# A Toeplitz product with only the corner blocks off the diagonal: 32x32 array tiles inside a stream of 128x128 passes

## The chip, the core and the metric

The kernel runs on one core of a Trainium2 chip. A core has a matrix engine (PE; its weight loads are shown as PEld), a vector engine (DVE), a scalar engine (ACT), GpSimd (POOL) and SyncE (SP), which run their own instruction streams and wait for each other by semaphores. Matmul results land in eight PSUM banks, `ps[0]` to `ps[7]`, each 128 partitions by 512 fp32. The metric is device time of one execution in microseconds (us), median of a few runs. A measurement of this kernel tells a change from no change at about 0.3%.

## The reference, cut to what matters

The whole program is a chain of small blocks (a deformable convolution, a Fourier-domain convolution, a Nystrom attention, a mixture of experts, a linear attention, a routed transformer). The change is in the Nystrom attention, in its residual term: a convolution of the values `v` along the tokens, one filter of 33 taps per head.

```
v: (b, h, n, dh), here 8 images, 8 heads, 256 tokens, 16 columns per head
pad = 33 // 2
res = conv_general_dilated(v, res_w, padding=((pad, pad), (0, 0)), feature_group_count=h)
out = a1 @ pinv(a2) @ (a3 @ v) + res          # pinv: 6 Newton-Schulz steps
```

Token i of `res` takes tokens i-16 to i+16 of `v`. With the 256 tokens in two blocks of 128, block t of the result needs all of block t of `v`, and of the other block the 16 tokens next to the border.

## The kernel before

Everything is written out by hand, engine by engine, in the order in which each engine executes it; semaphores `S[...]` tie the streams together. There is no scheduler: an engine that waits holds all that stands behind it.

The convolution is done as a matrix product. `toepb[:, h, 0:384]` holds head h's banded Toeplitz matrix (128 partitions, three column blocks of 128); block t of the result from block s of `v` uses its columns `(1 - t + s) * 128` on. The result comes out with its tokens reversed, which is undone later (`turn_residual`, line 776, with a flip matrix). The moving operand is `Vb[:, :, s, head]`, 8 images x 16 columns = 128 columns.

On PE, lines 743 to 749: for each t, each head h, each s one 128x128 product of 128 columns. That is 2 x 8 x 2 = 32 products. Every fp32 product is two passes in the trace, so there are 64 passes. Bank `ps[2t + h//4]` holds four heads; the banks complete in the order 0, 1, 2, 3, each with `res_mm` + 1.

On ACT, lines 1166 to 1170, a loop of four turns: wait for `a1_sub`, take the exponential of one 512-column piece of `a1` (line 1169), then `residual(n)` waits for `res_mm`, copies bank n out of PSUM (line 1159) and signals `res_ev`. Behind the loop stand four small scalings (`linear_term`, line 1164), and behind them the copies of the first Newton-Schulz step (line 1178), which DVE waits for.

On DVE, lines 1526 to 1533, a loop of four turns makes `a1_sub` (a maximum, line 1529, and a subtraction, line 1530, on banks 4 to 7) and from the second turn on sums the exponentials of the turn before (lines 1523, 1524). After it comes the Newton-Schulz step (lines 1547 to 1558).

On PE behind the residual products stands `pinv_step(0, ...)`: four groups of products (line 759) into banks 0 to 3, group q only when `res_ev` says that its bank has been copied out. Then line 765, which waits for DVE. The middle steps run in a loop, in which PE also turns a piece of the residual (line 776). GpSimd stages the first piece when `res_ev` is 4 (line 486).

Of the kernel before, what the change touches and what calls it, by code (L numbers as in the profile page):

```python
# [25 lines left out]
P = 128  # L26
BI, BG, PT = 4, 2, 2
# [3 lines left out]
HEADS, DH, LM = 8, 16, 16  # L31
# [93 lines left out]
def build(nc, x, cst, w32, par, rows, toep, w_out, moe_w1, moe_w2, moe_b2, am, fm, codes, rec_a, rec_b, out):  # L125
    ctx = ExitStack()
    with ctx:
# [3 lines left out]
        S = {n: ctx.enter_context(nc.semaphore(n)) for n in SEMS}  # L131
        ps = [ctx.enter_context(nc.psum_tensor(f"ps{i}", [P, 512], F32))[:, :] for i in range(8)]
# [76 lines left out]
        toepb = sb("toepb", HEADS * 384).rearrange("p (h n) -> p h n", h=HEADS)  # L209
# [311 lines left out]
        def _(pe):  # L521
            mm = nc.tensor.matmul
# [22 lines left out]
            for g in range(BG):  # L545
                for k in range(KK):
                    last = mm(ps[g][0:BI * NOFF, 0:N], off_bd[:, k, :, :], window(xnp, g, k // 3, k % 3, 16),
                              start=(k == 0), stop=(k == KK - 1))
                last.then_inc(S["off_mm"], 1)
            pe.wait_ge(S["off_ev"], BG)  # L550
            for t in range(PT):
                for g in range(BG):
                    c0 = (t * BG + g) * BI * NOFF
                    last = tr(ps[2][:, c0:c0 + BI * NOFF],
                              offC[0:BI * NOFF, g * N + t * P:g * N + t * P + P],
                              ident[0:BI * NOFF, 0:BI * NOFF])
# [4 lines left out]
            for r in range(BG * PT):  # L561
                for bi in range(BI):
                    if 0 < r <= PT:
                        pe.wait_ge(S["g_ev"], (r - 1) * BI + bi + 1)
                    elif r:
                        pe.wait_ge(S["g_evD"], (r - 1 - PT) * BI + bi + 1)
                    mm(ps[4 + bi][:, 0:KK * C], xn[:, r * P:r * P + P], dcn_bd[:, bi, :],
                       start=True, stop=True).then_inc(S["g_mm"], 1)
# [43 lines left out]
            for k in range(KK):  # L612
                for g in range(BG):
                    last = mm(ps[0][64 * g:64 * g + 64, 0:N], conv_bd[:, k, :, :],
                              window(xp, g, 3 * (k // 3), 3 * (k % 3), 16), start=(k == 0), stop=(k == KK - 1),
                              skip_group_check=True)
# [3 lines left out]
            for t in range(PT):  # L620
                last = tr(ps[2][:, t * P:t * P + P], feat[:, t * P:t * P + P], ident)
# [5 lines left out]
            for t in range(PT):  # L627
                last = mm(ps[3], featT[:, t, :], dft[:, t, 0:2 * N], start=(t == 0), stop=(t == PT - 1))
# [8 lines left out]
            for g in range(BG):  # L637
                for t in range(PT):
                    mm(ps[1][:, (t * BG + g) * P:(t * BG + g + 1) * P],
                       x1C[:, g * N + t * P:g * N + t * P + P], ident, start=False, stop=False,  # L640
                       skip_group_check=True)
            keep_busy(4)
            pe.wait_ge(S["gated"], 2)
            for a in range(2):
                for t in range(PT):
                    last = tr(ps[7][:, (a * PT + t) * P:(a * PT + t + 1) * P],
                              gated[:, a * N + t * P:a * N + t * P + P], ident)
            last.then_inc(S["fft_mm"], 1)
            pe.wait_ge(S["fft_ev"], FFT_EV["gT"])
            for n, (a, t) in enumerate(((0, 0), (0, 1), (1, 0), (1, 1))):  # L650
                last = mm(ps[2], gT[:, a, t, :], dft[:, t, a * N:a * N + 2 * N], start=(n == 0), stop=(n == 3))
# [4 lines left out]
            for n, src in enumerate((outf, gatef)):  # L656
                pe.wait_ge(S["abs"], n + 1)
                for t in range(PT):
                    last = mm(T1[:, t, :, n * CH:n * CH + CH], src[:, t * P:t * P + P],
                              ident.rearrange("p (b c) -> p b c", b=B), start=False, stop=True,  # L660
                              skip_group_check=True)
# [29 lines left out]
            for b in range(B):  # L691
                last = mm(ps[0][:, 16 * b:16 * b + 16], ql_bd[:, b, :, :], kl[:, b, :], start=True, stop=True)
            last.then_inc(S["sim2_mm"], 1)
            for bi in range(BI):
                pe.wait_ge(S["v_ev"], bi + 1)
                for g in range(BG):
                    last = mm(ps[4 + bi][:, g * N:g * N + N], ql_bd[:, 2 * bi + g, :, :],
                              kT[:, 512 * bi + N * g:512 * bi + N * g + N], start=True, stop=True)
                last.then_inc(S["sim3_mm"], 1)
            for bi in range(BI):  # L700
                pe.wait_ge(S["a3_exp"], bi + 1)
                for j in range(4):
                    last = tr(ps[4 + bi][:, j * P:j * P + P], a3[:, 512 * bi + j * P:512 * bi + j * P + P], ident)
                last.then_inc(S["a3T_mm"], 1)
            for bi in range(BI):
                pe.wait_ge(S["a3T_ev"], bi + 1)
                for g in range(BG):
                    b = 2 * bi + g
                    for t in range(PT):
                        c0 = 512 * bi + (g * PT + t) * P  # L710
                        last = mm(ps[2 + b // 4][:, (b % 4) * P:(b % 4) * P + P], a3T[:, c0:c0 + P],
                                  V[:, c0:c0 + P], start=(t == 0), stop=(t == PT - 1))
# [3 lines left out]
            for b in range(B):  # L716
                last = tr(ps[b // 4][:, (b % 4) * P:(b % 4) * P + P], bdX[:, b, :, :], ident)
# [4 lines left out]
            for half in range(2):  # L722
                pe.wait_ge(S["xT_ev"], half + 1)
                for j in range(4):
                    b = half * 4 + j
                    last = mm(ps[half][:, j * P:j * P + P], bdXT[:, b, :, :], bdXT[:, b, :, :],
                              start=True, stop=True)
                last.then_inc(S["y0_mm"], 1)
            pe.wait_ge(S["cr_in"], 1)
            for bi in range(BI):  # L730
                for g in range(BG):
                    for t in range(PT):
                        c0 = 512 * bi + g * N + t * P
                        last = mm(ps[4 + bi][:, (g * PT + t) * P:(g * PT + t + 1) * P], qT[:, c0:c0 + P],
                                  kl_bd[:, 2 * bi + g, :, :], start=True, stop=True)
# [3 lines left out]
            Vb = V.rearrange("p (b t n) -> p b t n", b=B, t=PT)  # L739
            pe.wait_ge(S["y_bd"], 2)  # L740
            pe.wait_ge(S["w3_ev"], 1)
            for t in range(PT):
                for h in range(HEADS):
                    for s in range(PT):
                        col = (1 - t + s) * P
                        last = mm(ps[2 * t + h // 4][:, (h % 4) * P:(h % 4) * P + P], toepb[:, h, col:col + P],
                                  Vb[:, :, s, h * DH:h * DH + DH], start=(s == 0), stop=(s == PT - 1))
                    if h % 4 == 3:
                        last.then_inc(S["res_mm"], 1)

# [2 lines left out]
            def pinv_step(it, meanwhile, bank_free=lambda q: None):  # L753
                for q in range(4):
                    bank_free(q)
                    pe.wait_ge(S["y_bd"], it * 4 + 3 + q)
                    for j in range(2):
                        b = 2 * q + j
                        last = mm(ps[q][:, 160 * j:160 * j + 160], bdY[:, b, :], YV[:, b, :], start=True, stop=True)  # L759
                    last.then_inc(S["yy_mm"], 1)  # L760
                meanwhile(it)
                for q in range(4):
                    pe.wait_ge(S["rest_set"], it * 4 + 1 + q)
                    for j in range(2):
                        last = mm(ps[q][:, 320 + 64 * j:384 + 64 * j], bdY2[:, 2 * q + j, :, :],  # L765
                                  pG[:, 2 * q:2 * q + 2, :], start=True, stop=True)
                    last.then_inc(S["wy_mm"], 1)
# [17 lines left out]
                                  ident)  # L785
                    last.then_inc(S["a1T_mm"], 1)

            pinv_step(0, nothing, lambda q: pe.wait_ge(S["res_ev"], q + 1))
            pe.wait_ge(S["a1_sub"], BI)
            with pe.Fori(1, PINV - 1) as it:  # L790
                pinv_step(it, turn_residual)
# [2 lines left out]
            for b in range(B):  # L794
                pe.wait_ge(S["y_bd"], 4 * PINV + 3 + b // 2)
                last = mm(ps[b // 4][:, (b % 4) * P:(b % 4) * P + P], bdZ[:, b, :, :], w3_bd[:, b, :, :],
                          start=True, stop=True)
# [3 lines left out]
            for bi in range(BI):  # L801
                pe.wait_ge(S["w2_ev"] if bi < 2 else S["w2_evD"], 1)
                pe.wait_ge(S["a1T_ev"], BI)
                for g in range(BG):
                    b = 2 * bi + g
                    last = mm(ps[4 + bi][:, g * N:g * N + N], w2_bd[:, b, :, :], a1T[:, N * b:N * b + N],  # L806
                              start=True, stop=True)
                last.then_inc(S["oT_mm"], 1)
            pe.wait_ge(S["late_in"], LATE)
            for bi in range(BI):  # L810
                pe.wait_ge(S["oT_ev"], bi + 1)
                last = mm(ps[0][32 * bi:32 * bi + 32, :], woutb, oT[:, 512 * bi:512 * bi + 512],
                          start=True, stop=True)
            last.then_inc(S["ao_mm"], 1)
            pe.wait_ge(S["ao_ev"], 1)
            for g in range(BG):
                for t in range(PT):
                    last = mm(ps[2][:, (t * BG + g) * P:(t * BG + g + 1) * P],
                              lnC[:, g * N + t * P:g * N + t * P + P], ident, start=False, stop=True,
                              skip_group_check=True)  # L820
# [8 lines left out]
            for g in range(BG):  # L829
                last = mm(ps[1][64 * g:64 * g + 64, 0:N], gate_bd, lnC[:, g * N:g * N + N], start=True, stop=True)  # L830
# [5 lines left out]
            for t in range(PT):  # L836
                last = tr(ps[3][:, t * P:t * P + P], probs[:, t * P:t * P + P], ident)
# [3 lines left out]
            for b in range(B):  # L841
                for t in range(PT):
                    j = t * B + b
                    last = mm(ps[4][0:C, 16 * b:16 * b + 16], t0[:, j * C:j * C + C], mT[:, t, 16 * b:16 * b + 16],
                              start=(t == 0), stop=(t == PT - 1))
# [5 lines left out]
            for e in range(EXP):  # L851
                q, c = e % 4, e // 4
                last = mm(ps[5][32 * q:32 * q + B, HID * c:HID * c + HID], pooled[:, B * e:B * e + B],
                          w1b[:, HID * e:HID * e + HID], start=True, stop=True)
# [3 lines left out]
            for c in range(4):  # L858
                last = tr(ps[6][:, c * P:c * P + P], hid_rows[:, c * P:c * P + P], ident)
# [3 lines left out]
            for e in range(EXP):  # L863
                last = mm(ps[4][0:C, B * e:B * e + B], w2b[:, C * e:C * e + C], hid[:, e, 0:B],
                          start=True, stop=True)
# [17 lines left out]
            for g in range(BG):  # L883
                for t in range(PT):
                    c0 = (t * B + g * BI) * C
# [166 lines left out]
        def _(act):  # L1052
# [101 lines left out]
                   scale=small[:, 34:35]).then_inc(S["y_bd"], 1)  # L1154
            rr4 = res.rearrange("p (t b h e) -> p t h b e", t=PT, b=B, h=HEADS)

            def residual(n):
                act.wait_ge(S["res_mm"], n + 1)
                af(rr4[:, n // 2, 4 * (n % 2):4 * (n % 2) + 4],
                   ps[n].rearrange("p (h b e) -> p h b e", h=4, b=B), ACT.Copy).then_inc(S["res_ev"], 1)  # L1160

# [4 lines left out]
            for bi in range(BI):  # L1166
                act.wait_ge(S["a1_sub"], bi + 1)
                v = a1[:, 512 * bi:512 * bi + 512]
                af(v, v, ACT.Exp).then_inc(S["a1_exp"], 1)
                residual(bi)  # L1170
            act.wait_ge(S["z0_set"], 1)
            for q in range(4):
                linear_term(0, q)
# [1 line left out]
            def pinv_step(it, meanwhile, last_one):  # L1175
                for q in range(4):
                    act.wait_ge(S["yy_mm"], it * 4 + 1 + q)
                    af(bdY2[:, 2 * q:2 * q + 2].rearrange("p b h m -> p b (h m)"),
                       ps[q][:, 0:320].rearrange("p (b c) -> p b c", b=2)[:, :, 0:P], ACT.Copy
                       ).then_inc(S["yy_ev"], 1)  # L1180
                meanwhile(it)
                if not last_one:
                    for q in range(4):
                        linear_term(it + 1, q)
# [645 lines left out]
```

## Time and profile before

| | |
|---|---|
| median of 3 runs | 342.33 us (341.65 to 342.83) |
| the profiled execution: device time | 342.63 us |
| its span, first to last instruction | 340.8 us |
| mean granted TensorE clock | 0.988 |
| PE busy | 301.4 us (88%), 2034 matmul passes |
| DVE busy | 195.4 us (57%) |
| ACT busy | 159.2 us (47%) |
| the 64 passes of line 746 | 7.3 us, 144.27 to 151.6 us |

The profile gives busy time per engine, groups of instructions per line, the chain of work that ended last, and the instructions in order of time. Three things are to be kept in mind. A matmul pass is pipelined: its row lasts some 0.27 us, but in a stream the next one starts 0.11 us later, so the start times say more than the durations. A busy PE does not mean that PE sets the time. And a chain names, for each step, what came last before it; whoever is not in it had time to spare, how much has to be read from the other engines' rows.

### The profile page before, as it was taken

The numbers are of one execution on the slowest core, as the hardware profiler recorded it, in microseconds if no ns is written. First come the engines' busy times: TensorE is split into PE (matmuls) and PEld (weight loads), VectorE is DVE, ScalarE is ACT, GpSimd is POOL, SyncE is SP. The second block draws the span as 40 slices with busy tenths as digits, with TensorE's granted clock in tenths as the row PEclk, the third lists the DMA queues.
The fourth block names the chain that finished last, engine by engine and source line by source line (L and its number), as shares of the span: only waits on it lengthen the run. The fifth ranks groups of instructions, "written<-read, shape, count | busy, mean of one in ns | idle before, by whom it ended". The sixth has DMA issues, their size and how long they took to land.

```text
span 340.8 us, 6667 instructions
## 1 busy us (share of the span) xinstructions
PE 301.4 (88%) x2034; PEld 199.1 (58%) x2034; DVE 195.4 (57%) x468; ACT 159.2 (47%) x346; POOL 37.6 (11%) x34
## 2 busy tenths in 40 slices
PE   7999999999889899999999989899986887777770
PEld 3665777776444358998998346588542552234420
DVE  4585998882165775688885652723512482228520
ACT  1097677776164267365662242112043495527820
POOL 5200190001000060001200000242000000000010
PEclk9999999999999999999999999999999799999997
DMA  3944100000000000000000233331000000000001
GB/s 90 251 102 112 56 0 2 2 2 0 2 0 0 1 2 0 2 0 2 1 0 0 40 66 61 68 68 35 2 3 20 2 0 0 17 17 0 0 15 35
DMA packets 9385, 9.17 MB, mean 27 GB/s; under 512 B 4079, under 2 KB 8943, under 8 KB 9071
## 3 DMA queue, kind: packets, MB, share of 16 engines
q1 hardware_dynamic: 9096, 8.53, 11.1%
q8 instruction: 15, 0.25, 0.3%
q10 hardware_dynamic: 264, 0.30, 0.3%
q14 instruction: 10, 0.08, 0.1%
HBM read 8.57 MB, written 0.26 MB: 26 GB/s over the span
## 4 chain that ended last, share of the span: by engine, by line
PE 30%; DVE 12%; issue 5%; ACT 4%; DMA 2%; DVEq 1%; SPq 0%; POOL 0%; POOLq 0%
PE ps L759 3%; PE ps L528 3%; PE ps L765 3%; DMA recA<-rec_a 2%; PE ps L915 2%; ACT arena L1255 2%; PE ps L1034 2%; DVE rmax L1706 2%; PE ps L905 1%; PE ps L1026 1%; PE ps L897 1%; PE ps L1004 1%; PE ps L776 1%; PE ps L806 1%; DVE arena L1530 1%
## 5 line engine op out<-in xcount | busy, mean ns | idle before, releaser
L528 PE MATMUL ps<-xC,cstb 128*128 128x512 f32 (+3 forms) x140 | 59.7, 554 | 0.0
L1375 DVE TENSOR_TENSOR arena<-arena 128x512 f32 x72 | 44.4, 688 | 7.8 <-ACT arena L1086 4.5
L1093 ACT ACTIVATE arena<-ps 128x512 f32<-128x512 f32 x72 | 37.7, 602 | 15.7 <-PE ps L585 15.6
L528 PEld LDWEIGHTS ps<-xC,cstb 128*128 128x128 f32 x140 | 24.6, 190 | 24.7 <-issue 24.6
L585 PE MATMUL ps<-cstb,arena 128*128 128x128 f32 x288 | 36.3, 277 | 0.7 <-DVE arena L1375 0.7
L585 PEld LDWEIGHTS ps<-cstb,arena 128*128 128x128 f32 x288 | 31.0, 140 | 9.4 <-DVE arena L1375 8.6
L593 PE MATMUL ps<-arena 128*32 128x256 f32 x288 | 19.2, 385 | 0.0
L1255 ACT ACTIVATE arena<-ps,rmax 128x256 f32<-128x256 f32 x32 | 14.9, 471 | 5.6 <-DVE rmax L1706 5.6
L1274 ACT ACTIVATE arena<-ps,w2c 128x512 f32<-128x512 f32 x16 | 9.7, 689 | 12.9 <-PE ps L1026 12.9
L759 PE MATMUL ps<-arena 128*128 128x160 f32 x96 | 14.5, 304 | 0.3 <-DVE arena L1558 0.3
L996 PE MATMUL ps<-cstb,arena 128*128 128x128 f32 x64 | 10.5, 286 | 4.4 <-DVE arena L1714 4.2
L1706 DVE TENSOR_REDUCE rmax<-ps 128x2 f32<-128x512 f32 x16 | 10.8, 684 | 5.8 <-PE ps L985 5.8
L497 POOL TENSOR_TENSOR arena<-w32b,cstb 128x1024 f32<-128x1024 f32 x4 | 7.6, 1895 | 57.5 <-PEq L891 45.8
L759 PEld LDWEIGHTS ps<-arena 128*128 128x128 f32 x96 | 13.3, 190 | 0.5 <-DVE arena L1558 0.4
L453 POOL TENSOR_SCALAR cgw<-cstb,parb 128x128 f32<-128x128 f32 x1 | 9.6, 9605 | 30.9 <-DMA codeB<-codes 30.9
L996 PEld LDWEIGHTS ps<-cstb,arena 128*128 128x128 f32 x64 | 6.7, 140 | 10.8 <-DVE arena L1714 10.8
L1034 PE MATMUL ps<-arena,w2c 128*32 128x512 f32 x32 | 11.1, 605 | 2.0 <-ACT arena L1274 2.0
L1061 ACT ACTIVATE small<-small 128x16 f32<-128x16 f32 x5 | 1.1, 216 | 23.3 <-DVE small L1301 22.3
L506 POOL TENSOR_TENSOR ln_a<-tC,hC 128x512 f32<-128x512 f32 x1 | 1.3, 1266 | 94.9 <-DVE hC L1734 94.9
L765 PE MATMUL ps<-arena,bdY 128*128 128x64 f32 x96 | 11.5, 273 | 0.3 <-DVE arena L1549 0.3
L765 PEld LDWEIGHTS ps<-arena,bdY 128*128 128x128 f32 x96 | 11.2, 192 | 0.5 <-DVE arena L1549 0.5
L992 PE MATMUL ps<-cstb 128*128 128x256 f32 x32 | 9.8, 387 | 1.9 <-ACT arena L1255 1.9
(374 smaller groups left out, 542.8 us busy)
## 6 DMA issues: line engine op xcount, KB each, us to landing
arena<-rec_a SPq DMA_DIRECT2D x19, 128.5 KB
toepb<-toep SPq DMA_DIRECT2D x1, 1536.0 KB
w32b<-w SPq DMA_DIRECT2D x1, 1225.0 KB
cstb<-cst SPq DMA_DIRECT2D x1, 1044.0 KB
recA<-rec_a SPq DMA_DIRECT2D x4, 128.5 KB
arena<-rec_b SPq DMA_DIRECT2D x19, 16.5 KB
w1b<-moe_w SPq DMA_DIRECT2D x1, 264.0 KB
xC<-x SPq DMA_DIRECT2D x1, 256.0 KB, 2.8
```

The costliest lines, as they stand in the source:

```text
L528: mm(ps[bank][:, 0:cols], ident if lhs is None else lhs, (xC if rhs is None else rhs)[:, 0:cols], start=True, stop=True)
L585: last = tr(ps[c % BI][:, (q * PT + t) * P:(q * PT + t + 1) * P], ST[:, c, t, q * 8:q * 8 + 8, :], ident)
L593: last = mm(ps[4 + g][32 * bi:32 * bi + 32, 0:N], GS[:, g, q, bi, k, :], SQ[:, g * BI + bi, q, :], start=False, stop=last_one and q == PT - 1,
L759: last = mm(ps[q][:, 160 * j:160 * j + 160], bdY[:, b, :], YV[:, b, :], start=True, stop=True)
L765: last = mm(ps[q][:, 320 + 64 * j:384 + 64 * j], bdY2[:, 2 * q + j, :, :], pG[:, 2 * q:2 * q + 2, :], start=True, stop=True)
L992: mm(ps[a][:, 0:N], ident, cstb[:, 0:N], start=True, stop=True)
L996: last = tr(ps[a][:, (u * PT + t) * P:(u * PT + t + 1) * P], pr[:, a * 512 + t * N + u * P:a * 512 + t * N + u * P + P], ident)
L1034: last = mm(ps[1][32 * bi:32 * bi + 32, :], w2c[:, 0:C], f1[:, 512 * bi:512 * bi + 512], start=True, stop=True)
L1093: af(SQ[:, c].rearrange("p q n -> p (q n)"), ps[c % BI], ACT.Copy).then_inc(S["s_ev"], 1)
L1255: last = af(pr[:, b * 512 + t * N:b * 512 + t * N + N], ps[b][:, t * N:t * N + N], ACT.Exp, bias=rmax[:, 2 * b + t:2 * b + t + 1], accum_o ...
L1375: tt_(ST[:, c], hy.unsqueeze(3).to_broadcast([P, PT, 16, 16]), hx.unsqueeze(2).to_broadcast([P, PT, 16, 16]), ALU.mult).then_inc(S["prod"], 1)
L1706: v_.tensor_reduce(rmax[:, 2 * b:2 * b + 2], arr3(ps[b], N), AX.X, ALU.max, negate=True).then_inc(S["sc_max"], 1)
```

## The change

The product of a whole off-diagonal block is replaced by a 32-row corner of it: of block 1-t only the 32 tokens `edge` next to the border are taken, and only the 32 rows of the result that can need them are written. The operands lie on 32 partitions, the result on 32 partitions: a tile of 32x32 of the matrix array, the one at rows and columns 0 to 31 for t = 0, the one at 96 to 127 for t = 1.

The loops are turned: head outside, then the two whole products (t = 0, 1) and then the two corners. So banks 0 and 2 fill together in heads 0 to 3, banks 1 and 3 in heads 4 to 7. ACT copies the banks out in the order 0, 2, 1, 3, still one per turn of its loop, and PE waits in the first Newton-Schulz step for `res_ev` of 1, 3, 3, 4 in place of 1, 2, 3, 4.

```diff
-            for t in range(PT):
-                for h in range(HEADS):
-                    for s in range(PT):
-                        col = (1 - t + s) * P
-                        last = mm(ps[2 * t + h // 4][:, (h % 4) * P:(h % 4) * P + P], toepb[:, h, col:col + P],
-                                  Vb[:, :, s, h * DH:h * DH + DH], start=(s == 0), stop=(s == PT - 1))
+            for h in range(HEADS):
+                cols = slice((h % 4) * P, (h % 4) * P + P)
+                for t in range(PT):
+                    mm(ps[2 * t + h // 4][:, cols], toepb[:, h, P:2 * P], Vb[:, :, t, h * DH:h * DH + DH],
+                       start=True, stop=False, skip_group_check=True)
+                for t in range(PT):
+                    edge = slice(96 * t, 96 * t + 32)
+                    c0 = (2 - 2 * t) * P + edge.start
+                    last = mm(ps[2 * t + h // 4][edge, cols], toepb[edge, h, c0:c0 + 32],
+                              Vb[edge, :, 1 - t, h * DH:h * DH + DH], start=False, stop=True, skip_group_check=True)
                     if h % 4 == 3:
                         last.then_inc(S["res_mm"], 1)
 
-            pinv_step(0, nothing, lambda q: pe.wait_ge(S["res_ev"], q + 1))
+            pinv_step(0, nothing, lambda q: pe.wait_ge(S["res_ev"], (1, 3, 3, 4)[q]))
 
-            def residual(n):
-                act.wait_ge(S["res_mm"], n + 1)
+            def residual(turn, n):
+                act.wait_ge(S["res_mm"], turn + 1)
...
-                residual(bi)
+                residual(bi, (0, 2, 1, 3)[bi])
```

On PE, the residual products of before, with the banks they write (each row is that many products, two passes each):

```order
L734 MATMUL ps7<-kl_bd,arena 128x128 x4
L746 MATMUL ps0<-arena,toepb 128x128 [waits w3_ev,y_bd,late_in]
L746 MATMUL ps0<-arena,toepb 128x128 x7
L746 MATMUL ps1<-arena,toepb 128x128 x8
L746 MATMUL ps2<-arena,toepb 128x128 x8
L746 MATMUL ps3<-arena,toepb 128x128 x8
L759 MATMUL ps0<-arena 128x160 [waits y_bd,res_ev,z0_set]
```

And the same place after the change, its first two heads (line 745 is the whole product, line 750 the corner; eight such groups of four follow each other, the last four on banks 1 and 3):

```order
L745 MATMUL ps0<-arena,toepb 128x128 [waits w3_ev,y_bd,late_in]
L745 MATMUL ps2<-arena,toepb 128x128
L750 MATMUL ps0<-arena,toepb 32x128
L750 MATMUL ps2<-arena,toepb 32x128
L745 MATMUL ps0<-arena,toepb 128x128
L745 MATMUL ps2<-arena,toepb 128x128
L750 MATMUL ps0<-arena,toepb 32x128
L750 MATMUL ps2<-arena,toepb 32x128
```

The number of products stays at 32; half of them are now corners, and the stream changes between whole-array products and 32-row tiles fifteen times, a sixteenth time where line 759 of before follows.

On ACT, the loop of four turns before:

```order
L1169 ACTIVATE arena<-arena 128x512 [waits a1_sub]
L1159 ACTIVATE arena<-ps0 128x4x8x16 [waits res_mm]
L1169 ACTIVATE arena<-arena 128x512 [waits a1_sub]
L1159 ACTIVATE arena<-ps1 128x4x8x16 [waits res_mm]
L1169 ACTIVATE arena<-arena 128x512 [waits a1_sub]
L1159 ACTIVATE arena<-ps2 128x4x8x16 [waits res_mm]
L1169 ACTIVATE arena<-arena 128x512 [waits a1_sub]
L1159 ACTIVATE arena<-ps3 128x4x8x16 [waits res_mm]
L1164 ACTIVATE arena<-arena 128x64 [waits v_new,z0_set]
```

And after:

```order
L1173 ACTIVATE arena<-arena 128x512 [waits a1_sub]
L1163 ACTIVATE arena<-ps0 128x4x8x16 [waits res_mm]
L1173 ACTIVATE arena<-arena 128x512 [waits a1_sub]
L1163 ACTIVATE arena<-ps2 128x4x8x16 [waits res_mm]
L1173 ACTIVATE arena<-arena 128x512 [waits a1_sub]
L1163 ACTIVATE arena<-ps1 128x4x8x16 [waits res_mm]
L1173 ACTIVATE arena<-arena 128x512 [waits a1_sub]
L1163 ACTIVATE arena<-ps3 128x4x8x16 [waits res_mm]
L1168 ACTIVATE arena<-arena 128x64 [waits v_new,z0_set]
```

The rows are the same but for the bank: the third copy takes bank 1, and so stands ahead of the fourth exponential with a bank that fills only in PE's last four heads.

## Rows read from the trace of the kernel before

**Rows 1.** Chain of waits, 143 to 157 us: start us, us, what.
```profile
144.27 0.70 DVE small L1529
...
149.26 0.60 DVE small L1523
...
150.82 0.70 DVE arena L1530
...
151.54 0.10 ACT arena L1169
...
152.08 0.58 ACT arena L1159
...
153.24 0.28 ACT bdY L1178
...
153.62 0.22 DVE arena L1547
```
**Rows 2.** ACT in order of time: start us, us, what, count [idle before <-releaser].
```profile
146.26 0.60 ACT L1159 ACTIVATE arena<-ps 128x512 f32<-128x512 f32 x1
147.04 0.63 ACT L1169 ACTIVATE arena<-arena 128x512 f32<-128x512 f32 x1 [0.19 <-DVE arena L1530]
148.05 0.60 ACT L1159 ACTIVATE arena<-ps 128x512 f32<-128x512 f32 x1 [0.37 <-PE ps L746]
...
151.54 0.63 ACT L1169 ACTIVATE arena<-arena 128x512 f32<-128x512 f32 x1 [1.11 <-DVE arena L1530]
152.08 0.58 ACT L1159 ACTIVATE arena<-ps 128x512 f32<-128x512 f32 x1
152.56 0.68 ACT L1164 ACTIVATE arena<-arena 128x64 f32<-128x64 f32 x4
153.14 1.19 ACT L1178 ACTIVATE bdY<-ps 128x256 f32<-128x256 f32 x4
```
**Rows 3.** PE in order of time, 135 to 200 us.
```profile
144.27 7.31 PE L746 MATMUL ps<-arena,toepb 128*128 128x128 f32 x64
151.42 2.34 PE L759 MATMUL ps<-arena 128*128 128x160 f32 x16
154.03 2.00 PE L765 MATMUL ps<-arena,bdY 128*128 128x64 f32 x16 [0.27 <-DVE arena L1549]
156.34 2.59 PE L759 MATMUL ps<-arena 128*128 128x160 f32 x16 [0.31 <-DVE arena L1558]
```
**Rows 4.** Line 746 alone: count, duration ns min/median/max, first and last start.
```profile
L746 PE MATMUL ps<-arena,toepb x64: 275/275/275, 144.3 to 151.3; 128*128 128x128 f32 x64
```
**Rows 5.** PE, 57.7 to 58.1 us: whole passes (L585), then 32-column tiles (L593).
```profile
57.47 0.38 PE L585 MATMUL ps<-cstb,arena 128*128 128x128 f32 x2
57.78 0.64 PE L593 MATMUL ps<-arena 128*32 128x256 f32 x8
```
**Rows 6.** Lines 585 and 593 alone, one round.
```profile
L585 PE MATMUL ps<-cstb,arena x18: 272/273/330, 55.9 to 59.0; 128*128 128x128 f32 x18
L593 PE MATMUL ps<-arena x16: 379/379/403, 57.8 to 58.5; 128*32 128x256 f32 x16
```
**Rows 7.** PE, 205.5 to 205.9 us: tiles (L853), then a whole pass.
```profile
205.27 0.51 PE L853 MATMUL ps<-w1b,pooled 33*8 33x128 f32 x12
205.71 0.59 PE L528 MATMUL ps<-xC,cstb 128*128 128x384 f32 x1
```
**Rows 8.** Line 853 alone.
```profile
L853 PE MATMUL ps<-w1b,pooled x32: 269/269/273, 204.7 to 205.5; 33*8 33x128 f32 x32
```
**Rows 9.** PE, 190.5 to 191.05 us: the first three whole passes after an idle stretch.
```profile
190.67 0.60 PE L818 MATMUL ps<-cstb,lnC 128*128 128x128 f32 x3 [0.69 <-ACT lnC L1203]
```
**Rows 10.** PE, two idle stretches of the last part.
```profile
262.80 1.12 PE L968 MATMUL ps<-hC,arena 128*128 128x512 f32 x2 [2.57 <-DVE arena L1691]
...
303.16 1.12 PE L968 MATMUL ps<-hC,arena 128*128 128x512 f32 x2 [1.93 <-DVE arena L1691]
```
**Rows 11.** Two stretches: us, PE busy, granted clock, DMA share, GB/s.
```profile
262.00:269.00 7.00, 6.20 (x44) 0.76 0.01 2
302.00:309.00 7.00, 4.89 (x45) 1.00 0.00 1
```

## The prediction, made before the changed kernel ran

> **What bounds the kernel now.** I read the page first: PE is busy 88% of the span, so a change that takes 16 whole products off PE looks like a gain. Whether it is one, the chain of waits has to say, around 144 to 157 us. There PE does not appear at all [rows 1]: from 144.27 us the chain is DVE's loop (maximum, subtraction, sums), whose last subtraction starts at 150.82; it releases ACT's fourth exponential at 151.54, then ACT's fourth bank copy at 152.08, the four small scalings, the first copy of the Newton-Schulz step, and at 153.62 DVE again. The timeline of ACT says the same from the other side: before the fourth exponential ACT sat idle 1.11 us for DVE, and only one bank copy of the four waited for the residual products, 0.37 us at 148.05 [rows 2]. The timeline of PE shows the 64 passes from 144.27 and the next line at 151.42 [rows 3], so 7.15 / 64 = 0.1117 us a pass, though each lasts 0.275 us by itself [rows 4]. PE becomes the bound only at 156.34, where the Newton-Schulz loop begins. So a shorter residual on PE has nothing to give: the fourth exponential still waits for DVE at 151.54. It can only cost, if the banks come later than ACT asks for them.
>
> **How late ACT may get its banks.** A copy follows its exponential by 0.54 us, and the next instruction follows a copy by 0.48 us (151.54, 152.08, 152.56 [rows 2]). The fourth exponential stays at 151.54 if the third copy starts by 151.06. Before, the third copy took bank 2, the third in PE's order. Now it takes bank 1, which is complete only with the eighth and last head. From the start of a bank's last pass to ACT's copy: bank 1 of before had its 32nd pass at 144.27 + 31 x 0.1117 = 147.73, the copy started at 148.05 having waited for it [rows 2], 0.32 us. So the last head's corner must start by 150.74.
>
> **What a head costs PE now.** Before, four products, 8 passes, 0.893 us. Now 4 whole passes and 4 corner passes, with a change of array shape each way. No row of the trace has exactly this; the nearest are these.
> - Whole to tile: the last of the L585 passes starts at 57.47 + 0.38 - 0.27 = 57.58, the first tile pass at 57.78 [rows 5, 6]: 0.20 us, where in a stream it is 0.11.
> - The tile passes: eight passes of 256 columns on four column tiles; the last starts at 57.78 + 0.64 - 0.38 = 58.04, that is 0.26 after the first [rows 5, 6]. The tiles run side by side: in series eight would take 8 x 0.22. One 256-column pass is worth 0.22, so 0.04 is the first tile's load and the stagger. The twelve passes of L853, 128 columns, start within 0.51 - 0.27 = 0.24 us [rows 7, 8], two steps of 0.11 between three rounds of four. For two corners of 128 columns, two passes each: 0.11 + 0.03 = 0.14 from the first start to the last.
> - Tile to whole: the last L853 pass starts at 205.27 + 0.51 - 0.27 = 205.51, the whole pass at 205.71 [rows 7, 8]: 0.20.
> - The four whole passes: after a break the first one's weight load is not hidden. Of L818's first three passes the third starts at 190.67 + 0.60 - 0.275 = 190.995, 0.325 after the first [rows 9], and 0.11 of that is the second step: the first costs 0.213. First to fourth start: 0.213 + 2 x 0.112 = 0.437.
>
> One head: 0.437 + 0.20 + 0.14 + 0.20 = 0.977 us against 0.893. The halved array work is more than eaten by two changes of shape (0.09 above the stream's step each), the load no longer hidden (0.10), and the corners' own 0.14. The first head comes out of a running stream: last whole pass at 144.61, corners 144.81 to 144.95, the second head from 145.15. The eighth head's last corner: 145.15 + 6 x 0.977 + 0.437 + 0.20 + 0.14 = 151.79 us, 1.05 us later than ACT can bear.
>
> The Trainium skill bears on this at one place: "TensorEngine Tiling (Array Packing)", Key Properties, says that a change of tiling mode drains the engine, and its Overview gives 32x32 tiles a speedup of up to 16. By the speedup alone the corners would cost next to nothing and the time would stay at 342.3 (rival A below); by the drain the head grows. The page gives the drain no price; this trace does, about 0.09 us each way [rows 5 to 8].
>
> **The sum.** Third copy at 151.78 + 0.32 = 152.10 us; fourth exponential at 152.58 in place of 151.54: +1.04. Behind it stand on ACT the fourth copy (bank 3 long complete), four scalings and the copies for DVE, in unchanged distances, so DVE's 153.62 becomes 154.66. What else moves has time: the first copy (bank 0 complete in head four, last corner at 144.95 + 3 x 0.977 = 147.88) starts at 148.20 in place of 146.26, the second exponential at 148.68 in place of 147.04; it ends at 149.31, and DVE's second sum, at 149.2 before [rows 1], slips by 0.1 to 0.15 us, and with it the last subtraction, to 151.65: hidden below 152.58. PE goes on to line 759 at 151.98; group 0 finds its bank free, groups 1 and 2 wait for the third copy's end (152.7), group 3 for the fourth's (153.7), its last pass ends by 154.6; ACT needs it for its fourth copy at 153.14 + 0.79 + 1.04 = 154.97. Hidden. GpSimd's staging starts 1.0 later and its piece is used only after 158 us. From 154.66 on DVE and then PE run as before, all 1.04 us later.
>
> Profiled execution: 342.63 + 1.04 = 343.67. It lies 0.30 above the median of the runs, 342.33, so I give 342.33 + 1.04 = 343.4 us. I count as no change what is within 0.3%, 1.03 us: 341.30 to 343.36. The forecast lies on that edge.
>
> **Bounds.** Below: no head can make the time shorter, since DVE holds 151.54; the lowest end is a change of nothing. Above: if each corner pass were as isolated as the first pass of L818, four would cost 0.85 in place of 0.14 and 0.20, some 0.5 a head, 7 heads 3.6 us more: 347. I take 0.977, from the rows of tile passes, which are nearest.
>
> **Rivals.**
> A, not slower: the corners cost less than I think and ACT is never late. The point is exact: the last corner by 150.74 means (150.74 - 144.95) / 7 = 0.83 us a head. For it: a corner uses a sixteenth of the array, and all of my tile rows are of another shape (128 rows by 32 columns, 33 by 8). Against: it needs both drains and the load penalty halved, and both drains were the same 0.09 in two different shapes. Time 342.3.
> B: the two corners of a head don't run side by side (they differ in rows and in columns and write different banks, which no row shows together). Then two passes more in series, +0.21 a head; over seven heads 1.5 us, third copy 153.6, time 343.4 + 1.5 = 344.9. For it: nothing direct; against: column tiles overlap in rows 5 and 7.
> C: the granted clock falls once more. It fell after PE had been idle 2.57 us and stayed up after 1.93 us [rows 10]; the fall cost (1 - 0.76) x 7 = 1.7 us [rows 11]. In the new order PE's longest idle stretch here is some 0.5 us, but its array is less used. 343.4 + 1.7 = 345.1.
> D: everything after 154 us comes 1 us later, and the fall at 264 us doesn't happen in that execution: 343.4 - 1.7 = 341.7, no change. It can do so in either kernel.
>
> **How the numbers follow.** Forecast 0.66, its own range 342.9 to 343.9, half of it above 343.36. A 0.13, B 0.09, C 0.07, D 0.05. Slower: 0.33 + 0.09 + 0.07 = 0.49; same: 0.33 + 0.13 + 0.05 less what scatter takes out, 0.46; faster: 0.05, scatter of the medians alone. The range goes from 342.1 (A, with the medians' scatter) to 344.9 (B) and leaves out C, D and the far bound.
>
> **What would show it.** In the profile after: eight groups of about 0.98 us from line 745 and 750; the first idle of ACT before the first copy, until about 148.2, waiting for PE; ACT idle before the third copy, until about 152.1, waiting for PE, and none before the fourth exponential; the chain of waits going through PE's lines 745 and 750 at 145 to 152 us in place of DVE's loop; line 769's first pass at about 155.1. I am wrong if the fourth exponential still waits for DVE (A), if the heads take 1.19 (B), or if the time moves elsewhere than between 144 and 154 us.

## The result, and the profile after

The changed kernel took 344.14 us (median of 14 runs, 343.03 to 346.6) against 342.09 us of the kernel before in its 14 runs: ratio 1.0046, 95% interval 1.0023 to 1.0068, so 0.8 to 2.3 us slower. The forecast was 1.04 us slower, 343.4 us. Ratios leave out three runs, one of e2 and two of e4, that lay over 1.5% above the fastest of their kernel; the medians hold them. Its profiled execution took 343.58 us with a span of 341.8 us, 1.0 above the span of before, at nearly the same mean granted clock (0.989 to 0.988).

The chain of waits of the changed kernel, 143 to 158 us (start us, us, what), where [rows 1] had DVE's loop:

```profile
142.97 1.45 PE ps L734 x13
144.42 0.45 PE ps L745 x4
144.86 0.34 PE ps L750 x4
145.20 0.64 PE ps L745 x4
145.84 0.34 PE ps L750 x4
...
151.08 0.64 PE ps L745 x4
151.72 0.39 PE ps L750 x4
152.10 0.05 ACT arena L1163
152.15 0.43 issue
152.58 0.62 ACT arena L1173
153.20 0.49 ACT arena L1163
...
154.65 0.22 DVE arena L1551
```

The chain now runs through PE's residual, head by head, then through ACT's third bank copy and fourth exponential. ACT in order of time, the answer to [rows 2]:

```profile
145.71 0.63 ACT L1173 ACTIVATE arena<-arena 128x512 f32<-128x512 f32 x1 [3.32 <-DVE arena L1534]
148.17 0.60 ACT L1163 ACTIVATE arena<-ps 128x512 f32<-128x512 f32 x1 [1.83 <-PE ps L750]
...
152.09 0.60 ACT L1163 ACTIVATE arena<-ps 128x512 f32<-128x512 f32 x1 [1.80 <-PE ps L750]
152.58 0.62 ACT L1173 ACTIVATE arena<-arena 128x512 f32<-128x512 f32 x1
154.16 1.20 ACT L1182 ACTIVATE bdY<-ps 128x256 f32<-128x256 f32 x4
```

The copies that waited 0.37 us for PE in all now wait 1.83 and 1.80, and the fourth exponential, which had waited 1.11 us for DVE, waits for nobody: it stands behind the third copy and starts at 152.58 in place of 151.54. PE, the answer to [rows 3], two heads and the line behind:

```profile
144.25 0.61 PE L745 MATMUL ps<-arena,toepb 128*128 128x128 f32 x4
144.79 0.41 PE L750 MATMUL ps<-arena,toepb 32*32 32x128 f32 x4
145.13 0.71 PE L745 MATMUL ps<-arena,toepb 128*128 128x128 f32 x4
145.77 0.41 PE L750 MATMUL ps<-arena,toepb 32*32 32x128 f32 x4
146.11 0.71 PE L745 MATMUL ps<-arena,toepb 128*128 128x128 f32 x4
...
151.99 2.65 PE L763 MATMUL ps<-arena 128*128 128x160 f32 x16
155.06 2.00 PE L769 MATMUL ps<-arena,bdY 128*128 128x64 f32 x16 [0.43 <-DVE arena L1553]
```

A head takes 146.11 - 145.13 = 0.98 us where it had taken 0.893. Half of PE's 64 passes are now corners, and still its next line starts at 151.99 in place of 151.42.

### The profile page after: what moved, and what is told of

Same layout as the page of the kernel before. It is cut to its first block, busy times and chain, and to the rows that moved or that the text cites. A ratio compares the mean times of both kernels' runs of the same rounds, so it can differ in the third digit from the quotient of the medians.

```text
span 341.8 us, 6667 instructions
## 1 busy us (share of the span) xinstructions
PE 303.2 (89%) x2034; PEld 197.3 (58%) x2034; DVE 195.6 (57%) x468; ACT 158.9 (46%) x346; POOL 34.0 (10%) x34
## 4 chain that ended last, share of the span: by engine, by line
PE 69%; DVE 11%; ACT 9%; issue 5%; DMA 2%; DVEq 1%; POOL 1%; SPq 0%; POOLq 0%
PE ps L585 10%; PE ps L528 10%; PE ps L593 5%; PE ps L763 3%; PE ps L769 3%; DMA recA<-rec_a 2%; PE ps L547 2%; PE ps L919 2%; ACT arena L1259 2%; PE ps L1038 2%; DVE rmax L1710 2%; PE ps L745 1%; PE ps L909 1%; PE ps L1030 1%; ACT arena L1090 1%
## 5 line engine op out<-in xcount | busy, mean ns | idle before, releaser
L585 PE MATMUL ps<-cstb,arena 128*128 128x128 f32 x288 | 36.3, 277 | 0.7 <-DVE arena L1379 0.7
L585 PEld LDWEIGHTS ps<-cstb,arena 128*128 128x128 f32 x288 | 31.0, 140 | 9.4 <-DVE arena L1379 8.6
L593 PE MATMUL ps<-arena 128*32 128x256 f32 x288 | 19.2, 385 | 0.0
L1718 DVE TENSOR_TENSOR arena<-arena,rsum 128x512 f32<-128x512 f32 x16 | 11.1, 692 | 0.6
L593 PEld LDWEIGHTS ps<-arena 128*32 128x32 f32 x288 | 7.5, 109 | 6.3 <-ACT arena L1097 3.1
```

The lines of the kernel that those rows point to most:

```text
L585: last = tr(ps[c % BI][:, (q * PT + t) * P:(q * PT + t + 1) * P], ST[:, c, t, q * 8:q * 8 + 8, :], ident)
L593: last = mm(ps[4 + g][32 * bi:32 * bi + 32, 0:N], GS[:, g, q, bi, k, :], SQ[:, g * BI + bi, q, :], start=False, stop=last_one and q == PT - 1,
L1718: tt_(pb3, pb3, r.unsqueeze(2).to_broadcast([P, 2, N]), ALU.mult).then_inc(S["sc_norm"], 1)
```

## The experiments

All of them are read in two ways. One is the ratio of runs, which is blunt here. The other is two lengths out of the one profiled execution, both from the start of PE's first residual pass: to DVE's first Newton-Schulz step (line 1547 of before, "to DVE"), and to PE's products behind the last Newton-Schulz step (line 796 of before, "to the end of pinv"). In the kernel before they are 153.62 - 144.27 = 9.35 and 181.66 - 144.27 = 37.39 us [rows 1, 3]. The row of the second in the kernel before, and those of the changed kernel in its two profiles (the second profile's first residual pass is at 144.79):

```profile
181.66 2.09 PE L796 MATMUL ps<-w_bd,bdX 128*128 128x128 f32 x16
```
```profile
182.68 2.09 PE L800 MATMUL ps<-w_bd,bdX 128*128 128x128 f32 x16
```
```profile
183.23 2.09 PE L800 MATMUL ps<-w_bd,bdX 128*128 128x128 f32 x16
```

| kernel | to DVE | to the end of pinv | median us | ratio and interval |
|---|---|---|---|---|
| before | 9.35 | 37.39 | | |
| changed | 10.40 | 38.43 | 344.14 | 1.0046 (1.0023 to 1.0068) |
| e1, changed again | 10.39 | 38.44 | 342.98 | 1.002 (0.9985 to 1.0055) |
| e2, order alone | 9.46 | 37.50 | 343.02 | 1.0001 (0.997 to 1.0032) |
| e3, exponentials first | 10.00 | 38.21 | 343.30 | 1.0018 (0.999 to 1.0047) |
| e4, grouped | 9.34 | 37.37 | 342.71 | 0.9986 (0.995 to 1.0023) |
| e5, grouped, one start | 9.34 | 37.38 | 342.74 | 0.9998 (0.9974 to 1.0022) |
| e6, start early | 8.14 | 36.46 | 341.84 | 0.9966 (0.9937 to 0.9996) |
| e7, scalings early | 8.77 | 37.20 | 342.34 | 0.9982 (0.9956 to 1.0008) |
| e8, before again | 9.35 | 37.39 | 342.46 | 0.9985 (0.9956 to 1.0013) |
| e9, one corner | 10.35 | 38.38 | 340.6, one run | |
| e10, no corners | 9.33 | 39.38 | 347.98, one run | |
| e11, the same again | 9.37 | 39.52 | 345.53 | 1.010 (1.0047 to 1.0154) |
| e12, the same, filled | 9.35 | 37.39 | 342.21 | 0.9988 (0.9953 to 1.0024) |

**e1_after_again and e8_before_again**: both kernels unchanged.

> The changed kernel once more, beside the kernel before on the same chip. Its profile puts the loss at 1.04 us (DVE's first step of Newton-Schulz at 154.65 in place of 153.62), while the ratio of the runs gave 0.46%, 1.6 us. Theory P (all of it stands on the path between 144 and 154 us, the rest is scatter of the clock): ratio 1.003, between 1.002 and 1.005; over many runs the difference nears 1.04 us. Theory C (part of the loss, 0.5 us, is a TensorE clock that falls more often in the changed kernel): ratio 1.0045 or more, and a mean clock of its runs that is lower than that of the profiled one.

> The kernel before, unchanged, run as a kernel of its own, so that the granted clock of each of its runs is listed. Theory P: mean clock as that of the changed kernel's runs, 0.983, ratio 1.000. Theory C (the changed kernel's clock falls more often): its mean clock is higher, 0.986 or more, which is some 0.5 us at about 0.6 us a fall of 0.005.

The stage repeats to 0.01 us in both kernels; the rest of the span doesn't. All 26 runs of the changed kernel have a mean of 343.83 us, all 110 of the kernel before 342.68: a difference of 1.15 us with a standard error of 0.25. The clock is listed for 96 of the 110, not for the 14 of the first comparison; these 96 have a mean of 342.78 us and a mean granted clock of 0.9811, the changed kernel's 26 one of 0.9823. So theory C falls: the changed kernel's clock is no lower. The clock goes with most of the scatter: over both kernels a run is some 0.85 us longer for each 0.005 of mean clock less, and with that taken out the difference is 1.2 us, standard error 0.14. The first ratio of 1.0046, 1.6 us, was the high side of this scatter: the 14 runs of the kernel before in it had a mean of 341.94 us.

**e2_order_alone**: the changed order with whole products.

```diff
...
             for h in range(HEADS):
                 for t in range(PT):
...
+                    for s in range(PT):
+                        col = (1 - t + s) * P
+                        last = mm(ps[2 * t + h // 4][:, (h % 4) * P:(h % 4) * P + P], toepb[:, h, col:col + P],
+                                  Vb[:, :, s, h * DH:h * DH + DH], start=(s == 0), stop=(s == PT - 1))
```

> The changed order of heads, banks and copies, but both whole products for every block as before: 64 whole passes, no tile, no change of shape. Theory P: bank 1 is complete with the last head's pass 62, which starts at 144.25 + 61 x 0.112 = 151.07; third copy at 151.39, fourth exponential at 151.87 in place of 151.54: +0.33 us, ratio 1.001. Rival O (the order of banks is the whole loss, the changes of array shape cost nothing): fourth exponential at 152.6 and +1.0 us, ratio 1.003.

```profile
149.37 0.63 ACT L1169 ACTIVATE arena<-arena 128x512 f32<-128x512 f32 x1
151.24 0.60 ACT L1159 ACTIVATE arena<-ps 128x512 f32<-128x512 f32 x1 [1.24 <-PE ps L746]
151.74 0.62 ACT L1169 ACTIVATE arena<-arena 128x512 f32<-128x512 f32 x1
```

ACT in order of time: the third copy waits for PE here too, but only until 151.24, in a stage that began at 144.34. The order costs 0.11 us of the 1.04, less than the 0.33 expected; the expectation had counted bank 1's last pass as the 62nd, it is the 60th (144.34 + 59 x 0.1117 + 0.32 = 151.25), because bank 3 gets the last four. Rival O falls: the order gives ACT's wait its place, the shape changes give it its size.

**e3_exp_first**: the wait for bank 1 taken out from in front of the exponentials.

```diff
-                residual(bi, (0, 2, 1, 3)[bi])
+                if bi < 2:
+                    residual(bi, (0, 2)[bi])
+            residual(2, 1)
+            residual(3, 3)
```

> The changed kernel, but ACT takes its third and fourth exponential before the third bank copy (exponentials no longer stand behind the wait for bank 1). Theory P: the wait for PE at 152.09 is hidden behind the fourth exponential, which starts at 151.68 (DVE's last subtraction is 0.14 late); third copy 152.22, fourth 152.70, scalings 153.2 in place of 153.58 of the changed kernel: 0.4 us won back, +0.6 us against before, ratio 1.002. Rival S (PE's later stream itself sets the time, whatever ACT's order): no change against the changed kernel, +1.04 us, ratio 1.003.

To DVE 0.40 us are won back, as expected (10.00 against 10.40); to the end of pinv only 0.22. PE's last twelve passes of line 763 wait for ACT's third copy, which stands behind one more exponential here; they start 8.61 us into the stage (152.95 - 144.34), 0.12 later than in the changed kernel (152.74 - 144.25). PE goes from line 763 to line 769 with no idle time, the last pair of DVE's first step starts 0.30 us after the instruction before it (0.14 in the kernel before), and PE's next step starts 2.88 us after DVE's first step (157.22 - 154.34), 2.72 in the kernel before.

**e4_grouped and e5_grouped_one_start**: four changes of shape in place of sixteen.

```diff
...
+            for half in range(2):
+                for h in range(4 * half, 4 * half + 4):
...
+                        mm(ps[2 * t + half][:, cols], toepb[:, h, P:2 * P], Vb[:, :, t, h * DH:h * DH + DH],
+                           start=(h % 4 == 0), stop=False, skip_group_check=True)
+                for h in range(4 * half, 4 * half + 4):
...
+                        last = mm(ps[2 * t + half][edge, cols], toepb[edge, h, c0:c0 + 32],
+                                  Vb[edge, :, 1 - t, h * DH:h * DH + DH], start=False, stop=True,
...
```

The cut is e5's: it sets the start flag only on the whole products of the bank's first head, so that the corners add. e4 has `start=True` on every whole product, ahead of all corners of the bank, and its corners do not all add. The program's output is off by a relative 0.19, by more than with the corners left out altogether (0.07 in e10 below), which fits corners that replace what stands in their 32 rows. Which heads' corners do so was not looked at. e4 serves as a measurement of time alone.

> The changed kernel with the same 32 products, but per pair of banks first the eight whole products, then the eight corners: four changes of array shape in place of sixteen. Theory P: PE's residual ends near 150.1 in place of 152.0, bank 1 is ready for ACT at 150.2, the fourth exponential waits for DVE again at 151.54: the loss is gone and nothing is won, ratio 1.000 (0.998 to 1.002), the profile's line 1551 step of DVE at 153.6. Rival T (tiles of 32x32 are slow by themselves, not the changes): the corners take as long as before, the residual ends after 151.1 and some loss stays, ratio 1.001 to 1.003.

> The grouped order of before (eight whole products, then their eight corners, per pair of banks), now with the start flag only on the first whole product of each bank, so that the corners add to every head. Expected of the time: as the grouped kernel, stage length from PE's first residual pass to DVE's first Newton-Schulz step 9.34 us (9.35 in the kernel before, 10.40 in the changed one), ratio 1.000. If the start flag itself costs anything, the eight whole passes take longer than 1.88 us.

PE of e5 in order of time:

```profile
144.23 1.95 PE L746 MATMUL ps<-arena,toepb 128*128 128x128 f32 x16
146.11 1.06 PE L753 MATMUL ps<-arena,toepb 32*32 32x128 f32 x16
147.10 2.05 PE L746 MATMUL ps<-arena,toepb 128*128 128x128 f32 x16
149.08 1.06 PE L753 MATMUL ps<-arena,toepb 32*32 32x128 f32 x16
150.07 2.10 PE L767 MATMUL ps<-arena 128*128 128x160 f32 x12
```

Sixteen corner passes with the change back take 147.10 - 146.11 = 0.99 us; in the changed kernel four took 0.34 (145.13 - 144.79), eight times. The residual ends at 150.07. The loss is gone and nothing is won: DVE's loop is the bound again, as forecast for a shorter residual. Rival T falls. The rows give the other prices too: the first sixteen whole passes with the change to tiles take 146.11 - 144.23 = 1.88 us, 0.09 above sixteen steps of 0.1117, and the second sixteen, which come back from tiles, 149.08 - 147.10 = 1.98, another 0.10 for the load that is not hidden.

**e9_one_corner**: half of the corner work.

```diff
-                for t in range(PT):
+                for t in range(1):
                     edge = slice(96 * t, 96 * t + 32)
...
+                if h % 4 == 3:
+                    last.then_inc(S["res_mm"], 2)
```

> The changed kernel with the corner of t = 0 alone; the corners of t = 1 are left out, so block 1 of the residual lacks what it takes from block 0. Half of the corner work is gone, the changes of array shape stay at sixteen. Theory P (the changes and the load that they uncover cost, the corner work does not): a head still takes 0.97 us, 0.007 less than with two corners. Rival T (the tiles' own work costs): a head takes some 0.1 to 0.2 us less.

```profile
145.17 0.71 PE L745 MATMUL ps<-arena,toepb 128*128 128x128 f32 x4
145.81 0.40 PE L750 MATMUL ps<-arena,toepb 32*32 32x128 f32 x2
146.14 0.71 PE L745 MATMUL ps<-arena,toepb 128*128 128x128 f32 x4
```

A head still takes 0.97 us, after 0.98 with both corners. The second corner was free beside the first (this also settles rival B); what costs is going to the tiles and back, around the one corner that is left.

**e10_no_corners and e11_no_corners_again**: the corners left out; `for h`, `for t`, the whole product with `start=True, stop=True`, nothing else.

> The changed order with no corners at all: 32 whole passes, no change of shape; the residual lacks what each block takes from the other. PE's residual takes 32 x 0.112 = 3.6 us and ends at 147.8. Theory P: the stage from PE's first residual pass to DVE's first Newton-Schulz step is still 9.35 us as in the kernel before, since DVE's loop holds it: half of the passes of the kernel before were worth nothing. Rival: PE's part is worth something and the stage is shorter than 9.2 us.

> The kernel without corners once more, in many runs (the residual lacks what each block takes from the other). The single look had a stage of 9.33 us up to DVE's first step, as forecast, but the granted clock fell at 152.9 us, after PE had sat idle 1.9 and 0.9 us between 148.5 and 152.8, and the run took 348 us. Theory I (PE's idle time in this stage invites the fall): mean clock of the runs clearly below that of the kernel before (0.981), 0.970 or so, and ratio 1.005 or more although PE has 32 passes less to do. Theory N (the fall came by chance, as the falls elsewhere do): mean clock 0.981, ratio 1.000.

Up to DVE both were as forecast, 9.33 and 9.37 us. But both were slower than the kernel before by 2.0 to 2.1 us at the end of pinv, with 32 passes fewer. PE of e11 in order of time:

```profile
147.84 0.71 PE L758 MATMUL ps<-arena 128*128 128x160 f32 x4
150.47 1.35 PE L758 MATMUL ps<-arena 128*128 128x160 f32 x8 [1.93 <-ACT arena L1158]
152.72 1.19 PE L758 MATMUL ps<-arena 128*128 128x160 f32 x4 [0.90 <-ACT arena L1158]
154.04 3.68 PE L764 MATMUL ps<-arena,bdY 128*128 128x64 f32 x16
157.51 3.54 PE L758 MATMUL ps<-arena 128*128 128x160 f32 x16
```

Line 764's 16 passes take 3.68 us where they took 2.00 [rows 3]. The stretches of e11 (us, PE busy, granted clock, DMA share, GB/s):

```profile
148.50:152.80 4.30, 1.48 (x10) 1.00 0.00 0
152.80:159.70 6.90, 6.77 (x28) 0.52 0.00 0
```

PE, busy for 1.48 of 4.30 us, is given half of its clock (1.2 of 2.4 GHz) right behind, for nearly 7 us. The four timed runs of e11 had a mean clock of 0.972 against 0.982 of the kernel before on the same chip. Their median is 3.1 us above it, of which the stage explains 2.1. The rest lies elsewhere: e11's profile has one more half-clock stretch at 327 to 333.5 us, but so has e8's, at 327.5 to 331, so it need not follow from this stage.

**e12_no_corners_filled**: the idle time filled with products that nobody reads.

```diff
+            pe.wait_ge(S["a1_sub"], 1)
+            keep_busy(4, bank=4)
             pe.wait_ge(S["z0_set"], 1)
```

> The same, with four filler products of 512 columns (eight passes, 3.5 us, into bank 4, which nobody reads any more) behind the 32 residual passes, so that PE isn't idle between 148 and 151.5 us. Theory I: the mean clock is back at 0.981 and the ratio at 1.000, although PE does more work than without them. Theory N: mean clock and time as without the filler.

```profile
148.50:152.80 4.30, 4.30 (x17) 1.00 0.00 0
152.80:159.70 6.90, 6.18 (x46) 1.00 0.00 0
```

The same stretches of e12, whose stage begins 0.53 us later: the clock stays, and the end of pinv is back at 37.39 us. Its ten runs had a mean clock of 0.986 and a median 3.3 us below e11's; the slowest of them, 344.18 us, is faster than the fastest of e11, 345.45. Both leave the same products out, so theory I is shown: the idle time costs, by the clock. It also says why the whole off-diagonal products of the kernel before were no waste of time: they lay under DVE's loop and kept the clock. The corners do that as well; in the profiles of the changed kernel, e5 and e6 the clock in this stage is 1.00.

**e7_before_hoist**: the kernel before with ACT's four scalings in front of its fourth exponential.

```diff
+                if bi == 3:
+                    act.wait_ge(S["z0_set"], 1)
+                    for q in range(4):
+                        linear_term(0, q)
                 act.wait_ge(S["a1_sub"], bi + 1)
...
```

> The kernel before (all 64 whole passes, its bank order), with ACT's four scalings ahead of its fourth exponential, where it sat idle 1.11 us. Theory P: ACT's first Newton-Schulz copy moves from 153.14 to 152.56, but PE's 64 passes end at 151.3 and its four groups of line 759 at 153.76, so the fourth copy starts at 153.8 and DVE's fourth step gains only 0.15 us: ratio 0.9995 (no change that can be measured). Rival (the 0.58 us of scalings come off the path whole): ratio 0.998, -0.6 us.

To DVE 0.58 us are won, to the end of pinv 0.19: the long residual on PE now holds the fourth copy of the step, as expected.

**e6_start_early**: e5, and on ACT the fourth exponential behind the copies of the first step.

```diff
+                if bi < 3:
...
                 residual(bi, (0, 2, 1, 3)[bi])
...
-            pinv_step(0, lambda it: None, False)
+            pinv_step(0, last_exp, False)
```

> The grouped order, and on ACT the third and fourth bank copy and the four scalings ahead of the fourth exponential, which moves behind the four copies of the first Newton-Schulz step. Theory P (the shorter residual is worth something only if what follows no longer stands behind DVE's last subtraction): copies at 150.2 and 150.7, scalings to 151.7, first Newton-Schulz copy 151.73; DVE's first step starts as soon as its own loop ends, 152.5 in place of 153.6: -1.1 us, ratio 0.997. Rival (DVE's later parts or the fourth exponential take the time back): ratio 1.000.

ACT of e6, then its DVE, in order of time:

```profile
151.24 0.69 ACT L1172 ACTIVATE arena<-arena 128x64 f32<-128x64 f32 x4
151.82 1.41 ACT L1192 ACTIVATE bdY<-ps 128x256 f32<-128x256 f32 x4
153.13 0.62 ACT L1187 ACTIVATE arena<-arena 128x512 f32<-128x512 f32 x1
```
```profile
152.46 0.16 DVE L1561 SCALAR_TENSOR_TENSOR arena<-arena,ps 128x64 f32<-128x64 f32 x1
153.79 0.69 DVE L1537 TENSOR_REDUCE small<-arena 128x32 f32<-128x512 f32 x1 [0.17 <-ACT arena L1187]
```

DVE starts the step as soon as its own loop ends, 1.21 us earlier than in the kernel before. It gives 0.28 of them back: 0.17 waiting for the late exponential, the rest before the last pair of the step, on the way to PE's loop. 0.93 us remain at the end of pinv, and the interval of the ratio, 0.9937 to 0.9996, just leaves 1 out. This is the one version whose interval lies below the kernel before, with corners and a start flag as in e5. In its chain of waits PE's residual and line 767 are the bound:

```profile
149.91 0.33 PE ps L753 x6
150.24 2.59 PE ps L767 x16
```

So here, with DVE's last subtraction off the path, the length of the residual counts. How much of the 0.93 us the shorter residual gives and how much the order on ACT is not shown: the whole of that order was not run with the long residual, only the scalings (e7).

## Why the prediction was right

- What bounds: DVE's loop before, so that a shorter residual gives nothing. Shown by e5 and up to DVE by e10 (9.34 and 9.33 against 9.35).
- The head: 0.977 us worked out, 0.98 measured; the residual's last corner and line 763 at 151.79 and 151.98 forecast, line 763 at 151.99 measured. The two changes of shape and the uncovered load were the right terms: e5 has them one by one, and e9 has half of the corners and nearly the same head. Tiles of 32x32 paid at each change what tiles of other shapes had shown.
- ACT: third copy 152.10 forecast, 152.09 measured; fourth exponential 152.58 and 152.58; DVE's first step 154.66 and 154.65. DVE's slip of 0.1 to 0.15 was 0.14 (its second sum at 149.32 in place of 149.18 by the timeline) and stayed hidden.
- The point at which ACT starts to lose, a last pass at 150.74, was tried by e2: its 60th pass starts at 144.34 + 59 x 0.1117 = 150.93, in a stage that begins 0.07 us later than that of the kernel before, so 0.12 us too late, and the loss is 0.11. The 0.83 us a head that follows from this point for corners was not tried.
- The time: +1.04 forecast; +1.05 and +1.04 in the stage, +1.15 (standard error 0.25) in the means of 26 and 110 runs. The first set of runs alone gave +1.6, and its median, 344.14 us, lies above the forecast's own range of 342.9 to 343.9. It lies within the whole range, up to 344.9, whose upper end was drawn for B, which did not happen: that the first median is inside owes something to luck.
- Rivals: A falls by the profile after, B by its heads and by e9. C as put, a further fall in this stage of the changed kernel, did not come (the first row below: PE's clock was 1.00). But its mechanism is real, and e11 is what it looks like. D was right that the fall at 264 us can stay away, but not in the time: the changed kernel's profile has none behind the 2.57 us of idle time in the first routed layer, which in the kernel before were followed by one [rows 10], and has one of the same size in the second, after 1.89 us. (Both kernels have one more, over the last few microseconds.) What was underrated is how often falls differ between executions; the mean clock goes with some three quarters of the scatter between runs of one kernel.

```profile
142.00:153.00 11.00, 11.00 (x92) 1.00 0.00 0
302.59 1.12 PE L972 MATMUL ps<-hC,arena 128*128 128x512 f32 x2 [1.89 <-DVE arena L1695]
```

The Trainium skill's rule, in "TensorEngine Tiling (Array Packing)", Key Properties, that a change of tiling mode drains the engine, agrees with these traces: each change of shape costs 0.09 us above the stream's step, twice a head, and the head shrinks by only 0.01 us when half of the corner work goes.

## What to carry to other kernels

Work taken off an engine is worth what the chain of waits says of its last consumer, not its busy share; ask for each waiting instruction how late its input may come, and work out only the distance to that point. Small tiles in a stream of whole passes should stand together: count the changes of shape, not the products. And a start flag between a product and what is to be added to it must be looked at even when it is on other columns. And before idle time is made on PE, ask what keeps its clock.

## What the runs showed of the hardware that was not expected

- A stage in which PE lost 32 passes made the program 1% slower: 1.5 us of busy time in 4.3 us, with idle stretches of 1.93 and 0.90 us, were followed by half a clock for nearly 7 us in both profiles. That idle stretch is shorter than the 2.57 us of [rows 10], and of the length of the 1.93 there that had no fall behind it. So in these traces a fall can't be read off the length of the idle stretch before it.
- Sixteen corner passes with the change back take 0.99 us (e5). Eight steps of 0.11 are 0.88, sixteen would be 1.76: the two tiles, at opposite corners of the array and writing two banks, run side by side.
- e4 and e5 differ only in the start flags of whole products ahead of the corners. A head's own whole product carries the flag in the changed kernel too, and there its corner adds; what is new in e4 is a flag on other columns of the bank between the two. With it the output is off by 0.19. So the flag reaches beyond the columns written; how far was not tried. It costs no time; the stage is 9.34 us either way.
